# Gated attention: another order of the rounds, more gate buffers, value products and closings moved

## What is computed

```python
q = silu(x @ Wq); k = silu(x @ Wk); v = x @ Wv            # 16 heads of 64
log_alpha = -softplus(x @ Wa + ba)
cum = cumsum(log_alpha, axis=1)                            # per head, over the 512 tokens
decay = exp(where(causal, cum[i] - cum[j], -inf))
out = ((q @ k.T) * decay) @ v                              # with a scale
out = groupnorm(out) * gn_w + gn_b                         # per token and head
out = (out * silu(x @ Wg)) @ Wo
```

## Time and profile before

| what | us |
|---|---|
| median of 3 runs | 1564.95 (1564.88 to 1569.62) |
| profiled execution | 1571.91 |
| its span | 1570.2 |
| its mean granted TensorE clock | 0.915 |
| TensorE busy | 1273.0 (81%) |
| VectorE busy | 834.9 (53%) |
| ScalarE busy | 833.3 (53%) |
| GpSimd busy | 565.9 (36%) |

### The profile page before, as it was taken

The page is one execution under the profiler, slowest core; times in us unless marked ns, Lnnn a source line. Parts: engine busy times, 40 slices in busy tenths (PEclk is TensorE's granted clock), DMA queues, the critical chain, the costliest instruction groups (busy, mean ns, idle before and its releaser), DMA issues.

```text
span 1570.2 us, 22567 instructions
## 1 busy us (share of the span) xinstructions
PE 1273.0 (81%) x6808; PEld 742.1 (47%) x6838; DVE 834.9 (53%) x2632; ACT 833.3 (53%) x1893; POOL 565.9 (36%) x636
## 2 busy tenths in 40 slices
PE   5999999999999997987644957787888886786452
PEld 2444444444344335544424955566666664444242
DVE  3543453354444426467642347787676876557425
ACT  4777677677767734544312635565565663343121
POOL 2555455545545522221433552322223331112232
PEclk9999999999999999998776987999999997897686
DMA  7234322320000000000025841000000000000053
GB/s 205 56 76 88 56 56 55 55 78 1 1 1 1 1 1 0 1 1 1 14 94 144 248 126 41 1 2 0 1 1 1 1 1 27 1 1 7 21 151 97
DMA packets 77557, 67.28 MB, mean 43 GB/s; under 512 B 5025, under 2 KB 68641, under 8 KB 77185
## 3 DMA queue, kind: packets, MB, share of 16 engines
q1 hardware_dynamic: 73488, 57.69, 15.1%
q0 software_dynamic: 3520, 7.27, 1.3%
q10 hardware_dynamic: 432, 0.89, 0.2%
HBM read 37.42 MB, written 28.41 MB: 42 GB/s over the span
## 4 chain that ended last, share of the span: by engine, by line
PE 62%; DVE 19%; issue 8%; ACT 6%; SPq 2%; POOL 1%; DMA 1%; another core or an unknown queue 0%; POOLq 0%; ACTq 0%; DVEq 0%
PE bank L553 8%; PE bank L535 7%; PE bank L543 6%; PE bank L482 6%; PE bank L658 3%; PE bank L525 3%; PE bank L723 3%; PE bank L615 3%; PE bank L731 3%; PE bank L629 3%; PE bank L855 2%; DVE work L1388 2%; PE bank L644 2%; ACT work L995 1%; PE bank L823 1%
## 5 line engine op out<-in xcount | busy, mean ns | idle before, releaser
L1925 POOL TENSOR_TENSOR work<-work 128x512 f32<-128x512 f32 x256 | 266.5, 1041 | 271.2 <-DVE work L1396 271.2
L995 ACT ACTIVATE work<-bank,work 128x512 f32<-128x512 f32 x256 | 176.6, 690 | 116.7 <-DVE work L1388 116.5
L1388 DVE TENSOR_REDUCE work<-bank 128x1 f32<-128x512 f32 x256 | 176.7, 690 | 78.7 <-PE bank L535 77.9
L543 PEld LDWEIGHTS bank<-cst,work 128*128 128x128 f32 x1024 | 110.4, 141 | 164.1 <-issue 103.0
L543 PE MATMUL bank<-cst,work 128*128 128x128 f32 x1024 | 159.6, 283 | 6.5 <-ACT work L1003 6.3
L1396 DVE RECIPROCAL work<-work 128x1 f32<-128x1 f32 x256 | 41.9, 164 | 222.9 <-ACT work L995 222.6
L1003 ACT ACTIVATE work<-bank 128x512 f32<-128x512 f32 x256 | 152.7, 597 | 0.5 <-PE bank L543 0.5
L1965 POOL TENSOR_TENSOR work<-work 128x1232 f32<-128x1232 f32 (+1 forms) x32 | 55.5, 1735 | 257.6 <-DVE work L1467 257.5
L535 PE MATMUL bank<-work 64*128 64x512 f32 x512 | 144.5, 641 | 3.5 <-ACT work L995 3.4
L553 PE MATMUL bank<-work 128*64 128x512 f32 x512 | 137.4, 617 | 0.7 <-ACT work L1003 0.7
L2027 POOL TENSOR_SCALAR_AFFINE_SELECT work<-work 128x512 f32<-128x512 f32 x64 | 40.8, 638 | 228.2 <-ACT work L1206 228.2
(11 more groups left out here) (246 smaller groups left out, 2523.0 us busy)
## 6 DMA issues: line engine op xcount, KB each, us to landing
xs<-gat SPq DMA_DIRECT2D x18, 1040.0 KB, 11.6
W<-in_w SPq DMA_DIRECT2D x30, 322.0 KB
W<-in_w SPq DMA_DIRECT2D x23, 193.0 KB
work<-xs SPq DMA_DIRECT2D x62, 65.0 KB
gat<-yt SPq DMA_DIRECT2D x12, 256.0 KB, 3.4
work<-in_w SPq DMA_DIRECT2D x9, 322.0 KB
W<-in_v SPq DMA_DIRECT2D x1, 2048.0 KB, 11.7
x_ext<-in_x SPq DMA_DIRECT2D x4, 256.0 KB, 7.8
```

What stands on the lines that cost most here:

```text
L543: m = nc.tensor.transpose(out[:, k * P:(k + 1) * P], pA[u % 5][:, k * P:(k + 1) * P], ident)
L995: A(pA[u % 5], bank[u % 3][:, :], ACT.Exp, bias=nmax[:, u % 8:u % 8 + 1], accum_out=rsum[0][:, u % 8:u % 8 + 1]).then_inc(sem("a_e"), 1)
L1388: V.tensor_reduce(nmax[:, u % 8:u % 8 + 1], bank[u % 3][:, :], AX, ALU.max, negate=True)\
L1925: G.tensor_tensor(pA[u % 5], pA[u % 5], rsum[1][:, u % 8:u % 8 + 1].to_broadcast([P, S]), ALU.mult)\
```

## The change

The order of the rounds changes on TensorE, ScalarE and VectorE; GpSimd's list stays. The cores of the diff, with `...` for what is left out:

```diff
+        thE = [gat[:, i * S:(i + 1) * S] for i in range(4)]
...
+        CLOSE_AT = {0: (1, 0), 1: (1, 1), 2: (1, 2), 6: (2, 0), 7: (2, 1), 8: (2, 2), 10: (3, 0), 11: (3, 1), 13: (3, 2)}
+        TURN_AT = {3: 1, 9: 2, 14: 3}
+        V_MID = {3: (0, 1, 1), 4: (0, 1, 3), 6: (1, 0, 1), 7: (1, 0, 2)}
+        V_LATE = {2: (0, 1, 0), 3: (0, 1, 2), 7: (1, 0, 3)}
+        V_END = {5: (1, 0, 0)}
+
+        def th_buf(g):
+
+            if g < 12:
+                return thD[g % 8]
+            return (thE, thD[4:8], thD[0:4], thE, thD[4:8])[(g - 12) // 4][g % 4]
```

A key of the V tables is s, a value (batches ahead, half, token tile). TensorE:

```diff
                     if g + 1 < 32:
                         d_proj(g + 1, 0)
-                        d_proj(g + 1, 1)
                         d_decays(g + 1)
                         d_decay_to(g + 1, 0)
+                        d_proj(g + 1, 1)
                     if g < 32:
                         d_scores(g)
+                    value(V_MID, g)
+                    if more and s == ALPHA_AT[b]:
+                        d_alpha(b + 1)
                     if g + 1 < 32:
                         d_decay_to(g + 1, 1)
                     if 1 <= g <= 32:
                         d_proj(g - 1, 2)
                     if g < 32:
                         d_kturn(g)
+                    value(V_LATE, g)
+                    if more and s == SUMS_AT[b]:
+                        d_sums(b + 1)
                     if 2 <= g < 34:
                         d_out(g - 2)
+                    value(V_END, g)
...
```

Behind these the means and tails stand as before; `turn_x` follows TURN_AT; the values, alpha and sums at the end are gone. ScalarE (`d_decays` is cut into `d_el`, the first exponential, and `d_exps`, the four of one head; `d_affine` takes the pairs it does):

```diff
                     if g + 1 < 32:
                         d_tanh(g + 1, 0)
+                        d_el(g + 1)
+                        d_exps(g + 1, 0)
                         d_tanh(g + 1, 1)
-                        d_decays(g + 1)
+                    value(V_MID, g)
+                    if g + 1 < 32:
+                        d_exps(g + 1, 1)
                     if 1 <= g <= 32:
                         d_tanh(g - 1, 2)
+                    if more and s == ALPHA_AT[b]:
+                        d_softplus(b + 1)
+                    if s in (1, 5) and g >= 8:
+                        d_affine((g - 8) // 4, (2, 3))
+                    value(V_LATE, g)
                     if 2 <= g < 34:
                         d_o(g - 2)
+                    value(V_END, g)
                     if s in (0, 4) and g >= 8:
-                        d_affine((g - 8) // 4)
+                        d_affine((g - 8) // 4, (0, 1))
...
-                    if g >= 8:
+                    if 8 <= g < 12:
                         act.wait_ge(sem("d_og"), g - 7)
-                    A(thD[g % 8], src, ACT.Tanh, scale=0.5).then_inc(sem("d_th"), 1)
+                    elif g >= 16:
+                        act.wait_ge(sem("d_og"), g - 11)
+                    elif g == 12:
+                        act.wait_ge(sem("M_cb"), NB)
+                    A(th_buf(g), src, ACT.Tanh, scale=0.5).then_inc(sem("d_th"), 1)
```

VectorE:

```diff
+                    if g + 1 < 32:
+                        d_silu(g + 1, 0)
                     if 1 <= g <= 32:
                         d_st(g - 1)
                     if g + 1 < 32:
-                        d_silu(g + 1, 0)
                         d_silu(g + 1, 1)
                     if g < 32:
                         d_at(g)
+                    if more and s == ALPHA_AT[b]:
+                        d_z(b + 1)
+                    if g < 32:
                         d_kd(g)
...
-                    if s == 5 and b + 1 < NB:
+                    if more and s == (3 if b else 4):
                         d_split_x(b + 1)
+                    if g in CLOSE_AT:
+                        close_step(MOE[2], *CLOSE_AT[g])
+                    if s in (1, 5) and g >= 9:
+                        d_gated((g - 9) // 4, (0, 1, 2, 3))
                     if 2 <= g < 34:
                         d_stats(g - 2)
...
-                    if s in (1, 5) and g >= 9:
-                        d_gated((g - 9) // 4, (0, 1, 2, 3))
                     if g >= 16:
                         tail(PD + b - 2, s + 8)
-                    if g < 12:
-                        close_step(MOE[2], g // 4 + 1, g % 4)
...
```

More of the change, by code:

```diff
@@ L880, in phase_d, with value @@
                 d_decay_to(0, 1)
+                def value(at, g):
+                    if g < 32 and g % 8 in at:
+                        nb, hf, t = at[g % 8]
+                        if g // 8 + nb < NB:
+                            d_v(g // 8 + nb, hf, t)
                 for g in range(32 + 4):
                     b, s = g // 8, g % 8
+                    more = g < 32 and b + 1 < NB
                     if 1 <= g <= 32:
@@ L905, in phase_d @@
                         tail(PD + b - 2, s + 8)
[L906 to L921, removed]
+                    if g in TURN_AT:
+                        turn_x(PC + TURN_AT[g])
+                    if b and g < 32:
+                        tail(PD + b - 1, s)
             cross(1)
@@ L1196, in d_decays, with d_exps @@
                 A(elD[g % 3], bank[0][:, :], ACT.Exp, scale=-1.0).then_inc(sem("d_el"), 1)
[L1197 to L1208, removed]
+            def d_exps(g, hh):
+                b, p = g // 8, g % 8
+                if hh == 0:
+                    if p == 0:
+                        act.wait_ge(sem("d_lcs"), b + 1)
+                    if g >= 2:
+                        act.wait_ge(sem("d_at"), 2 * (g - 1))
+                act.wait_ge(sem("d_la"), 2 * g + hh + 1)
+                for c in range(NT):
+                    k = c * H + 2 * p + hh
+                    i = A(dmD[g % 2][:, (NT * hh + c) * P:(NT * hh + c + 1) * P], bank[1 - hh][:, c * P:(c + 1) * P],
+                          ACT.Exp, scale=-1.0, bias=lcD[b % 2][:, k:k + 1])
+                i.then_inc(sem("d_dm"), 1)
             def d_tanh(g, i):
@@ L1230, in d_o, with d_affine @@
                 A(o_slot(PD + g // 8, g % 8), bank[5][:, :], ACT.Copy).then_inc(sem("d_o"), 1)
-            def d_affine(k):
+            def d_affine(k, pairs):
                 act.wait_ge(sem("d_AB"), k + 1)
@@ L1236, in d_affine @@
                 b, p0 = k // 2, 4 * (k % 2)
-                for i in range(4):
+                for i in pairs:
                     o = o_slot(PD + b, p0 + i)
@@ L1250, in phase_d, with value @@
                 d_tanh(0, 1)
-                d_decays(0)
+                d_el(0)
+                d_exps(0, 0)
+                d_exps(0, 1)
+                def value(at, g):
+                    if g < 32 and g % 8 in at:
+                        nb, hf, t = at[g % 8]
+                        if g // 8 + nb < NB:
+                            d_v(g // 8 + nb, hf, t)
                 for g in range(32 + 4):
                     b, s = g // 8, g % 8
+                    more = g < 32 and b + 1 < NB
@@ L1282, in phase_d @@
-                d_affine(7)
+                    if g in TURN_AT:
+                        keep_xT(PC + TURN_AT[g])
+                    if b and g < 32:
+                        tail(PD + b - 1, s)
+                    if more and s == SUMS_AT[b]:
+                        d_kdec(b + 1)
+                d_affine(7, (0, 1, 2, 3))
             cross(1)
@@ L1834, in d_gated @@
                     o = o_slot(PD + b, p0 + i)
-                    V.scalar_tensor_tensor(out=o, in0=thD[p0 + i], scalar=1.0, in1=o, op0=ALU.add, op1=ALU.mult)\
+                    V.scalar_tensor_tensor(out=o, in0=th_buf(4 * k + i), scalar=1.0, in1=o, op0=ALU.add, op1=ALU.mult)\
                         .then_inc(sem("d_og"), 1)
@@ L1872, in phase_d @@
                         d_var((g - 7) // 4)
-                    if s in (1, 5) and g >= 9:
-                        d_gated((g - 9) // 4, (0, 1, 2, 3))
                     if g >= 16:
                         tail(PD + b - 2, s + 8)
-                    if g < 12:
-                        close_step(MOE[2], g // 4 + 1, g % 4)
-                    if g < 32:
-                        if b:
-                            tail(PD + b - 1, s)
-                        if b + 1 < NB:
-                            if s == ALPHA_AT[b]:
-                                d_z(b + 1)
-                            if s == SUMS_AT[b]:
-                                d_lsel(b + 1)
+                    if b and g < 32:
+                        tail(PD + b - 1, s)
+                    if more and s == SUMS_AT[b]:
+                        d_lsel(b + 1)
                     if s in (3, 7) and g >= 7:
```

23 lines of the change are left out of this document (3 added, 20 removed).

## The result

The changed kernel takes 1592.74 us (median of 4 runs, 1590.97 to 1599.81) against 1565.2 beside it: ratio 1.0175, interval [1.0143, 1.0206]. That is 27.5 us more where 6 were forecast, and above the range of 1550 to 1585. The profiled execution took 1599.81 (span 1598.1), 7.1 above the median, as the profile of before was.

The account below looks back on a forecast made before the run. TensorE was taken as the bound, winnable only in holes between its instructions. Holes +8.0 less 2 for the clock gave +6 us: 1577.9 profiled, 1571 as median; range 1550 to 1585.

Parts of the forecast that it names:

- The walked holes: TensorE's idle holes in the loop, summed by walking durations along each engine's order over four batches: together +8.0 us.
- I credit 2 us, between 0 and 10: Granted clock over the loop: longest holes shrink but new 2 us ones come as often, so 2 us are won.
- unlike 0.98: Sign of a wrong forecast: the third batch's mean clock grant differing from 0.98, or that batch under 87 us.
- The longest holes shrink: Clock step, TensorE in the loop: the longest holes get shorter, though new ones of 2 us come as often.
- the clock tips: Rival: three new holes a batch each followed by 3.4 us at half clock, 18 us more, 1587; chance 0.08.
- (a): Value products moved off the ends of s2, s3, s6, s7: TensorE waits 2.0 plus 0.6 in s7, 0.7 in s3/s4.
- (b): Decay sums ahead of the output: waits for their bank 2.0, then some 0.6; first batch about 2.9 us.
- (c): Gated products ahead of statistics in s1, s5: 2.6 us delay, projection waits 2.0 and 2.1; closings likewise in second batch.
- That hole goes: Affine in halves on ScalarE: exponential 1.5 us earlier, removing the decay product's 1.95 us hole.
- gone from round 16 on: Four more gate buffers: the gate tanh's 4.0 us wait and the projection's 1.67 behind it vanish from round 16.
- Activation of Q before the state update: VectorE order: a projection waits 1.3 us less, but the turn waits for the state update, giving 0.6 back.
- holes simply go: Rival: removed waits vanish with some 5 us of clock, -33, net -25 after value products, 1540; chance 0.25.

Follow-up runs that it names:

- a_bufaff: Kernel before plus four more gate buffers and the affines in halves: 1565.90 us, ratio 0.9995.
- all4_st: Changed kernel with gated products, sums, values and closings put back, and Q's activation again behind the state update: 1571.97 us, ratio 1.0021 to the kernel before.
- a_bas: Kernel before plus gate buffers, affine in halves and Q's activation ahead of the state update: 1558.82 us, ratio 0.9940.
- u_all4: Changed kernel with gated products, sums, values and closings all put back where they stood before: 1559.31 us, ratio 0.9946 to the kernel before.
- all4_inter: u_all4 with K's projection again ahead of the decay products and K's tanh ahead of the exponentials: 1553.11 us, ratio 0.9924 to the kernel before.
- u_3: Changed kernel with gated products, sums and closings put back, values left in the middle: 1559.12 us, ratio 0.9951 to the kernel before.
- u_sums: Changed kernel with the decay sums back at the round's end, behind the output: 1585.22 us, ratio 1.0107 to the kernel before.
- u_gated: Changed kernel with the gated products back behind the statistics on VectorE: 1579.76 us, ratio 1.0067 to the kernel before.
- u_close: Changed kernel with the expert layer's closings and the turns of x placed as before: 1583.34 us, ratio 1.0106 to the kernel before.
- fillh: Changed kernel plus 84 matmuls nobody reads, each fill covering half its hole: 1585.46 us, ratio 1.0097 to the kernel before.

## Why the prediction was wrong

The direction was right and the range was not. The sum had +8.0 for the holes and -2 for the clock; the two traces show +9.2, +12.2 and a third part, +5.7, that it did not have. Of the 21 us between 6 and 27.1 the clock's term is 14, the missing one 6, the holes 1. (With the clock at the 5 that the dummies tell, it is 7 and 13.)

**The walked holes: right as a sum.** Forecast for the four batches 16.6, 19.8, 16.6, 11.4; measured 19.1, 20.4, 14.4, 11.6. Change of the holes: forecast +8.0, measured +9.2. Third batch, s0 to s7: 2.8, 1.5, 3.0, 1.4, 1.7, 2.8, 2.8, 0.6 against 2.9, 1.1, 3.2, 1.3, 1.4, 1.9, 2.4, 0.4. It is 93.8 long where the sum said 88.7 + 4.5 = 93.2, but that is luck: its holes rose by 2.3, not 4.5, and clock (3.4 us at half clock became 6.8) and rest make up the difference. The total is helped by luck too: the first batch's holes fell by 0.6 where 3.2 was forecast, the third's rose by 2.2 less than forecast. State products of s5 to s6: 11.7 where 10.7 was forecast (8.7 before), of s0 to s1 10.7 where 10 was.

**The clock: the step that failed.** "I credit 2 us, between 0 and 10" is wrong in sign. The stretches at half clock grew from 34.1 to 58.0 us, their cost by 12.2 (some 5 by the dummies). The third batch's grant was 0.96, and "unlike 0.98" was the prediction's own sign of being wrong. "The longest holes shrink" held for the longest of all (4.6 became 3.0), not for the later batches, where 2.6 to 3.0 stand and 1.95 stood. Holes of 1.9 us or more went from 9 to 12 in the loop, stretches at half clock from 6 to 11. Of the eleven, two: the first follows the hole of 1.87 that ends at 1016.13 in round 5 (one of 2.66 lies inside it), the second the 1.92 of the sums' copy that ends at 1210.42:

```profile
1016.80:1030.50 13.70, 11.04 (x47) 8.19 (x44) 5.25 (x13) 3.22 (x9) 1.26 (x1) 0.50 0.01 1
1211.40:1214.80 3.40, 3.30 (x15) 1.88 (x15) 2.49 (x6) 2.71 (x8) 0.38 (x1) 0.50 0.00 0
```

Not each hole is followed so: five of the twelve are, within 1.5 us of their end, and the two of 3.00 (to 1178.76 and 1273.95) are not. What decides it isn't shown.

The rival "the clock tips", 0.08 and 1587, is the case that came nearest; its 18 us of clock on top of +6 was too much for the clock and too little for the rest. It should have had more of the chance: row 10 showed the drop behind 1.95, and the walk itself put three holes over 2 us in a batch. The other three batches' lengths show it: 93.0, 104.1 and 76.8 where the sum gives 85.8, 97.0 and 72.6, with the holes within 2.5 of the walk in each.

**The rest: left out.** 5.7 us lie in neither. The rest is 270.0 before, 270.4 in a_bufaff and 270.0 in all4_st, which has the interleaving; with Q's activation first it is 273.2 in a_bas and 274.5 in u_all4, and without the interleaving 273.0 (all4_inter); with the values in the middle 277.5 in u_3. So the activation's order goes with 3 to 5 us, the scattered values with 3, the interleaving with 1.5 at most. Part of it is waiting that the holes don't count: a product of 512 columns is recorded 0.40 us long though the next starts 0.23 behind it, so a wait behind one is some 0.17 longer than its hole, and there are nine more holes after than before. The remainder isn't explained. "No matmul is added or removed, so the time moves only with those holes and with the clock" was too simple.

**(a) values.** The 2.0 + 0.6 in s0 came as 2.63 + 0.22, and goes if the values go back. As a cost of the placement it was wrong all the same: the old place has a wait of its own, 3.2 behind var. Net nothing that can be told.

**(b) sums and (c) gated products and closings.** Right in place, too small in size: the statistics were 3.4 late, not 2.6, since four products took 3.58 (and 3.00 already before, where the prediction put 2.6); the x copy 3.0, not 2.0. Undone, they give 11 (sums), 17 (gated products) and 11 us (closings). For the first two that is more than their holes (9 us each in the loop), and half clock goes with them: 58.0 us become 51.2 in u_sums and 44.4 in u_gated. For u_close it is 61.8, no less, and the 9.7 of holes are most of its gain.

**The removals.** "That hole goes" and "gone from round 16 on" were right for the named waits (exponential 3.6, under the 4 forecast; no gate tanh wait), wrong as worth: alone they are 0. "Activation of Q before the state update ... 0.6 is given back" had the price and missed that it is what lets the others pay. The activation is worth nothing alone (1.0006) and 0.55% with buffers and affine (0.9995 to 0.9940). The rival "holes simply go" with -33 was three to four times too high: the edits that remove give 9 us by themselves (a_bas), and softplus, exponentials and interleaving together add nothing that can be told from it (u_all4, 0.9946 beside 0.9940).

**Number or length of the holes.** Holes rose from 47 to 56 and the clock fell, which agrees with the sentence of the Trainium skill that frequent micro-idles make it oscillate ("TensorE: Matmul & The Clock Gate", "A second HAM failure mode: psum-queue depth-cycling"). But a_bas has 51 holes and only 23.9 us at half clock, with 46.9 us of holes in place of 65.6, and fillh, with dummies in its holes, has 62 holes and 10.2. By these rows it is not the number of holes; their length comes nearer, though no single measure orders all the runs (40.3 us of holes in u_all4 go with 30.7).

## What to carry to other kernels

Before work is moved ahead of a long product, look which late work of another engine that product covered: three such moves cost 11 to 17 us each by the ratios, all four 36. A bank or buffer with two releasers needs both made early; each alone may measure as nothing, so try them together before dropping either. And give holes of 2 to 3 us a second price, for the half clock that can follow: here it followed five of twelve, and the half clock that the change added cost 5 to 12 us beside the 9 of its holes.

## What was not expected of the hardware

- Dummy matmuls in the holes make both kernels faster, 0.5% before, 0.8% after, with the granted clock of the loop from 0.95 to 1.00 and 0.92 to 0.99; 72 and 84 do as well as 133 and 161.
- Recorded durations understate what half clock does. A product of 512 columns is 0.40 us long at full and 0.63 at half clock, 1.6 times; from start to start it is 0.23 and 0.43, 1.83 times (below, 1210.72 on and 1212.77 on), and 1.95 times in the turn (0.11 and 0.21). With these the clock's cost of the table is some 1 to 2 us less in each kernel.

```profile
1210.72 0.40 PE L826 MATMUL bank<-W_low 128*128 128x512 f32 x1
1210.96 0.40 PE L827 MATMUL bank<-W_low 128*128 128x512 f32 x1
...
1212.77 0.63 PE L826 MATMUL bank<-W_low 128*128 128x512 f32 x1
1213.20 0.63 PE L827 MATMUL bank<-W_low 128*128 128x512 f32 x1
```

- A gated product on VectorE takes 0.68 us, but 1.77 when GpSimd's product of Q and `elD` (L2069, 1.26 us alone) runs beside it for 1.2 us: that is the 3.58 of round 17. Before, 0.65 us of that product beside it made the first 1.20, which is the 3.00 of the earlier trace rows. In round 13 it went the other way: the four took 2.49 and L2069 3.26. The rows show one of the two held up, not both slowed a little.
- How the clock's cost by the trace (12.2 us) and by the dummies (5 us) go together is only argued here; no run separates them.
